# Decoder layer, cross-attention: the three score banks run on across batches

## What is computed

```python
def _L0_xattn_ref(q, k, v, gamma):          # per batch: q, k, v are (128, 512)
    h = 8                                    # N_HEAD, 16 rows each
    qh = q.reshape(B, h, dq, Lq); kh = k.reshape(B, h, dq, Lk); vh = v.reshape(B, h, dv, Lk)
    qk = jnp.einsum('bhdq,bhdl->bhql', qh, kh) * scale        # scale = 1/4
    sm = jax.nn.softmax(qk, axis=-1)                          # 512 x 512 per head
    ret = jnp.einsum('bhql,bhdl->bhdq', sm, vh)
    return gamma * ret.reshape(B, Dv, Lq)
```

## Time and profile before

| | us |
|---|---|
| median of three runs (lowest, highest) | 1818.55 (1813.82, 1830.88) |
| time of the profiled execution | 1817.9 |
| its span, from first to last instruction | 1816.0 |
| self-attention, about 0 to 608 us | 608 |
| cross-attention, about 608 to 1308 us | 700 |
| feed-forward, about 1308 to 1816 us | 508 |

### The profile page before, as it was taken

How to read it: one execution, slowest core, us unless ns; L and a number is a source line. 1 busy time by engine, 2 the same in 40 slices (tenths; PEclk the granted TensorE clock), 3 DMA queues, 4 the chain that set the end, 5 groups by cost and what they waited for, 6 DMA issues and landing times. The chain is left out here.

```text
span 1816.0 us, 35158 instructions
## 1 busy us (share of the span) xinstructions
PE 1609.2 (89%) x11937; PEld 874.9 (48%) x12000; DVE 1523.5 (84%) x1894; ACT 1329.7 (73%) x2821; POOL 1090.9 (60%) x1532
## 2 busy tenths in 40 slices
PE   6999999999998789999999999999858777777774
PEld 5777777777776333333333333333324333333332
DVE  5778888887887888999999899999568898989885
ACT  4666645555454478888888788888778888888893
POOL 6667667676765433255543555422467888888862
PEclk9999999999999699999999999999988888888887
DMA  4465443434346363445456554444233333333311
GB/s 146 140 193 166 130 116 118 130 104 139 107 128 178 101 118 94 118 116 120 109 158 162 152 126 115 109 118 118 90 117 97 112 106 113 105 107 109 111 47 41
DMA packets 119269, 217.10 MB, mean 120 GB/s; under 512 B 32241, under 2 KB 34705, under 8 KB 116785
## 3 DMA queue, kind: packets, MB, share of 16 engines
q1 hardware_dynamic: 110770, 213.64, 41.9%
q0 software_dynamic: 8320, 1.21, 0.4%
HBM read 137.67 MB, written 76.02 MB: 118 GB/s over the span
## 5 line engine op out<-in xcount | busy, mean ns | idle before, releaser
L969 DVE TENSOR_REDUCE b_smax<-wide 128x2 f32<-128x1024 f32 x512 | 620.6, 1225 | 63.4 <-PE wide L1029 51.3
L945 ACT ACTIVATE b_prob<-bank 128x512 f32<-128x512 f32 x1024 | 555.9, 599 | 113.0 <-PE bank L1076 103.6
L1076 PE MATMUL bank<-b_xs,b_cs 50*128 50x512 f32 x1024 | 329.5, 478 | 23.4 <-ACT b_prob L945 12.4
L1059 PE MATMUL sums<-b_prob,b_vT 128*32 128x256 f32 (+1 forms) x3584 | 318.7, 427 | 5.6 <-ACT b_prob L945 0.5
L1029 PE MATMUL wide<-b_cs,b_xs 48*128 48x512 f32 x1024 | 282.8, 437 | 9.1 <-DVE b_smax L969 7.7
L1076 PEld LDWEIGHTS bank<-b_xs,b_cs 50*128 50x128 f32 x1024 | 133.4, 187 | 233.9 <-ACT b_prob L945 170.7
L885 POOL TENSOR_SCALAR b_max_part<-b_neg_max 16x128 fp32r<-16x128 f32 x64 | 18.4, 288 | 325.2 <-ACT b_neg_max L936 325.2
L370 ACT ACTIVATE a_prob<-wide,a_neg_max 128x128 f32<-128x128 f32 x512 | 181.5, 417 | 2.5 <-DVE a_neg_max L461 2.5
L1986 PE MATMUL wide<-c_w,c_xqT 128*128 128x512 bf16 x482 | 159.3, 503 | 7.5 <-issue 7.5
L895 POOL DMA_DIRECT2D b_xs<-b_max_part x256 | 133.6, 527 | 42.1 <-POOL b_max_part L888 37.3
L1059 PEld LDWEIGHTS sums<-b_prob,b_vT 128*32 128x32 f32 x3584 | 72.8, 108 | 165.0 <-issue 107.5
(11 more groups left out here) (156 smaller groups left out, 3342.8 us busy)
## 6 DMA issues: line engine op xcount, KB each, us to landing
scratch_c_part<-a_c_part SPq DMA_DIRECT2D x64, 256.0 KB
scratch_x_part<-a_x_part SPq DMA_DIRECT2D x64, 256.0 KB
b_xs<-scratch_x_part SPq DMA_DIRECT2D x128, 128.0 KB, 3.1
b_cs<-scratch_c_part SPq DMA_DIRECT2D x128, 128.0 KB, 3.1
scratch_heads<-b_heads SPq DMA_DIRECT2D x64, 256.0 KB, 2.5
a_xT<-in_xT SPq DMA_DIRECT2D x32, 256.0 KB, 6.4
a_c_in<-in_ctx SPq DMA_DIRECT2D x32, 256.0 KB, 2.6
a_x<-in_x SPq DMA_DIRECT2D x32, 256.0 KB, 4.1
```

The lines of the kernel that those rows point to most:

```text
L945: act.activation(prob[k % 8][:, :], e_ps[bank_of(k)][:, :], ACT.Exp, scale=0.25).then_inc(exp_done, 1)
L969: dve.tensor_reduce(smax[g][:, :, j, qc], m_ps[u % 2][:, :, :], AX.X, ALU.max, negate=True).then_inc(max_done, 1)
L1059: last = pe.matmul(av_ps[2 * XD * h:2 * XD * (h + 1), cols], vT[p][:, lc, XG * g + h, :], prob[(XG * n + 2 * j + e) % 8][:, cols], start=( ...
L1076: pe.matmul(e_ps[bank_of(2 * u + e)][:, :], cs[p][g][half(e), j, lc * P:(lc + 1) * P], xs[p][g][half(e), j, :], start=True, stop=True).the ...
```

## The change

It touches two things and no instruction's place. The bank of a score unit is now counted through all batches, `bank_of(32 * t + k)`, on both sides (PE's matmul and ACT's exponential). The wait ahead of a pair or unit is the same formula for all: the first pair of a batch `t` waits for `exp_done >= 32 * t - 1`, so for all exponentials made before but the last one (unit 31 of the batch before); before it was `32 * t`. All other waits come out with the numbers they had. In the very first batch the count is not positive and there is no wait, as before. The lists of all five engines hold the same instructions in the same order, with waits on the same semaphores; one number per batch differs, and the bank addresses of batches whose 32 * t is not a multiple of 3.

```diff
-                    act.activation(prob[k % 8][:, :], e_ps[bank_of(k)][:, :], ACT.Exp, scale=0.25).then_inc(
+                    act.activation(prob[k % 8][:, :], e_ps[bank_of(UNITS * t + k)][:, :], ACT.Exp, scale=0.25).then_inc(
                         exp_done, 1)
...
-            free = max(2 * u + halves[-1] - 2, 0)
-            if free > 0 or not first:
-                pe.wait_ge(exp_done, UNITS * t + free)
+
+            free = UNITS * t + 2 * u + halves[-1] - 2
+            if free > 0:
+                pe.wait_ge(exp_done, free)
             for e in halves:
-                pe.matmul(e_ps[bank_of(2 * u + e)][:, :], cs[p][g][half(e), j, lc * P:(lc + 1) * P],
+                pe.matmul(e_ps[bank_of(UNITS * t + 2 * u + e)][:, :], cs[p][g][half(e), j, lc * P:(lc + 1) * P],
                           xs[p][g][half(e), j, :], start=True, stop=True).then_inc(score_done[e], 1)
```

## The result

The changed kernel took 1814.56 us in the median of 22 runs (1802.17 to 1829.51). The kernel before, run beside it, took 1826.07 us in the median of 22 (1813.82 to 1843.09; the three runs shown ahead of the prediction are among them). The ratio is 0.9941, with a 95% interval of 0.9916 to 0.9965: the kernel is faster by 0.6%. The ratios in this document are estimates from the single runs, those far above the fastest of their kernel left out; they can lie up to 0.003 away from the quotient of the two medians. The profiled execution of the changed kernel took 1802.17 us, the fastest of its 22, with a span of 1800.3.

What follows compares the result with a forecast made beforehand. PE in the cross-attention was taken as the bound; 26 batch starts at 0.48 us sum to 12.5 us, which off the median 1818.55 gives 1806.0 us, with a range of 1799 to 1815.

Steps and rivals of the forecast that it cites:

- What bounds the kernel: Cross-attention: PE is nearest to full, busy 670.2 of 700 us; its scores waited 12.4 us for exponentials in 28 waits.
- The price of the wait: At each of 26 batch starts, no longer waiting for the last exponential saves 0.48 us.
- The reading from the middle of the batch: Between steps 3 and 4, unit 4n+2 to next pair takes 1.28 us, against 1.76 at the batch's start.
- the idle column: Alternative measure from PE's idle time at batch starts: 26 x 0.45 = 11.7 us; the prediction used measured starts instead.
- What is late next: At a batch start the maxima's DMAs, step 7's products, DVE and ACT were checked; none was expected to hold PE.
- DVE's cover of 0.05 us: At a batch start DVE's reductions would end 0.05 us before the earlier plain scores; two buffers would hide slight lateness.
- The banks: Score banks change their number only; cost 0.
- The sum against the level of the runs: 26 x 0.48 = 12.5 us, taken off the three-run median 1818.55, gives 1806.0; a gain of 11 to 14 had chance 0.76.
- The five held places at gain 0: Five batch starts set by landings of the maxima's DMAs keep their time: gain 0, or up to 2.4 us if landings came earlier.
- a slower kernel: Rival: longer idle at held places lowers TensorE's clock, about 3.3 us each; four falls give 1819; chance 0.03.
- all held places would pay: Prediction's reading of the skill's rule: work after every DMA wait starts at half clock; trace agreed for batches 3 and 19.

Runs made afterwards that it cites:

- e2: Changed kernel with the full wait for all exponentials put back at each batch start, new banks kept: 1824.97 us, ratio 0.9983 to the kernel before.
- e3: Changed kernel with the full wait at the start and in the middle of every batch: 1842.26 us, ratio 1.0061 to the kernel before.
- e4: Changed kernel with the full wait ahead of the pair of all eight steps of a batch: 1891.72 us, ratio 1.0358 to the kernel before.
- e13: Changed kernel with the full wait back at each batch start, loads where they were, in the four-kernel job: 1820.83 us, ratio 0.9988 to the kernel before.
- e1: The changed kernel itself run again, in the job of the added full waits: 1813.10 us, ratio 0.992 to the kernel before.
- e9: Changed kernel with seven large loads sent one per batch and the feed-forward's first loads moved into batch 30: 1799.29 us, ratio 0.9842 to the kernel before.
- e14: The kernel of e9 (all large loads apart, new wait) run again in the four-kernel job: 1799.04 us, ratio 0.9875 to the kernel before.
- e10: The kernel of e9 with the full wait put back at each batch start: 1817.29 us, ratio 0.9953 to the kernel before.
- e15: The kernel of e10 (all large loads apart, old wait) run again in the four-kernel job: 1813.08 us, ratio 0.9943 to the kernel before.
- e12: The changed kernel run again in the four-kernel job, loads where they were: 1817.34 us, ratio 0.9959 to the kernel before.
- e7: Changed kernel with the weights' sums moved from GpSimd's DMA queue to SyncE's, large loads left in place: 1809.56 us, ratio 0.989 to the kernel before.
- e8: e5 and e7 together, large loads apart and the weights' sums by SyncE's queue: 1804.17 us, ratio 0.9863 to the kernel before.
- e6: The kernel of e5 with the full wait put back at each batch start: 1823.84 us, ratio 0.9984 to the kernel before.
- e5: Changed kernel with seven 1 MB feed-forward loads sent one per batch in batches 12 to 18: 1804.65 us, ratio 0.9872 to the kernel before.

## Why the prediction was right and wrong

**What bounds the kernel: right.** PE in the free batches, with one wait of 0.45 us of idle time, 0.48 to 0.50 by the starts. The waits that e2 and e3 add measure 0.50 and 0.49; only the eight of e4 cost less, 0.38 each.

**The price of the wait: right.** 0.48 was taken; the free periods went from 21.34 us to between 20.84 and 20.88. The reading from the middle of the batch (1.28 us from unit 4n+2 to the pair) came true to the digit. Going by starts rather than by the idle column was right too: the idle column would have said 0.45.

**What is late next: right.** Maxima, products, DVE and ACT all kept up at the free places; DVE's cover of 0.05 us was enough: from the first scores to the last the profile of the changed kernel lists one wait of PE for DVE, of 0.40 us in batch 0.

**The banks: right.** e2 against the kernel before: 0.9983 and, as e13, 0.9988, both with 1 inside the interval.

**The sum against the level of the runs: wrong, and this is the step that failed in absolute terms.** The prediction set 1806.0 by taking 12.5 us off 1818.55, "so the median after is 1806.0". The median of three runs was not the kernel's level: over 22 runs it is 1826.07, and over the other jobs' runs 1823.6 to 1828.7. From 1826.07 the same sum gives 1813.6, and 1814.56 was measured. Of the 8.6 us between 1806.0 and 1814.56, 7.5 are the level and 1.0 is the gain. That 1814.56 still lies inside the range of 1799 to 1815, by 0.4 us, is luck. The measured ratio of 0.9941 and the forecast one, 1806.0 over 1818.55 or 0.9931, agree within the interval. The gain over 22 runs, 11.5 us, is just short of the 12.5 forecast; the runs cannot tell these two apart. The three runs had a spread of 17 us, and the prediction used it for the range but not for its centre.

**The five held places at gain 0: the second weak step, its size open.** The prediction let them keep their time, because "neither end moves against the other". The waits there do move, in either kernel: over batches 14 to 19 those for the maxima's DMAs add up to 4.5, 4.2 and 4.2 us in three traces with the old wait and to 3.9, 4.8, 5.3 and 5.3 in four with the new one. What they cost moves more, by the clock, which the prediction had named as what makes such a wait dear and given 0.03 as the cause of a slower kernel. Slower it never was. Over these six batches its sum has a gain of 1.4 us (three free places); the traces show a loss of 3.3 on average, and a gain of 0.6 if e1 is left out. At the lower clock PE spent 6.8 us of these batches in each of the three traces with the old wait, and 0, 47.8, 13.7 and 13.7 us in the four with the new one. So that the falls are more frequent or longer with the new wait rests on four traces against three, of which one carries most.

The times say more. Over the single runs of all jobs the means are 1815.6 us (46 runs, new wait) and 1824.3 (24, old) with the loads where they were, 8.7 apart, and 1800.3 (12) and 1816.1 (24) with all of them apart, 15.8 apart. With 95% intervals from the scatter of the runs these are 8.7 within 3.4 and 15.8 within 3.5, so the gains differ by 7.1 within 4.9 us. With the 114 runs of the kernel before put to the old wait, the first is 10.4 within 2.4 and they differ by 5.4 within 4.3. About 1.7 us of either difference are plain: three or four more places gain 0.49 each. What is left for the held places to give back is 5.4 within 4.9 us or 3.7 within 4.3, with chips and jobs mixed in it: likely, and not shown. Why the landings should come later with the shorter batches is argued, not shown: the same bytes now share a shorter batch.

**Open.** With the loads apart the gain of the new wait came out at 14.0 to 19.2 us, where 29 or 30 places at 0.49 make 14.2 to 14.7. The traces show where the surplus is not. From the start of batch 4 to the start of batch 31 the kernels with all loads apart take 563.3 us with the new wait (e9 and e14) and 576.7 and 576.6 with the old (e10 and e15): 13.3 apart, 27 places at 0.49. And the longer idle time costs no clock there, which was e10's rival; e14 and e15:

```profile
700.00:1270.00 570.00, 564.44 (x4874) 215.67 (x4872) 542.18 (x492) 506.45 (x984) 257.25 (x378) 1.00 0.51 128
700.00:1270.00 570.00, 552.71 (x4753) 210.65 (x4753) 530.03 (x482) 494.19 (x960) 255.56 (x377) 1.00 0.51 126
```

What differs beyond that lies outside: over the 17 traces the stage up to the first scores, which no edit touches, took 608.2 to 622.4 us, and batch 0 took 22.3 to 30.3. So medians of 6 to 12 runs that scatter by some us are the nearest explanation; that it is only this, these runs don't settle.

## What to carry to other kernels

A wait that repeats inside a loop can be priced in the old trace, by finding a place in the same loop where the same list of instructions runs without it, and measuring from start to start. Before forecasting an absolute time, ask how well the runs know the level: here three runs were 7.5 us off, more than half of the effect. And look at the few places where the engine that bounds waits for a DMA: clearing them was worth another 14 us (1813.10 in e1, 1799.29 in e9, in two jobs) to 18 us (1817.34 in e12, 1799.04 in e14, side by side).

## What the runs showed of the hardware that was not expected

Many short idle times of PE don't lower its clock, one longer one may. Waits of PE and the window of 570 us in e4:

```profile
PE bank L1079 <- ACT b_prob L945: 81.0, 247, 0.5
```
```profile
700.00:1270.00 570.00, 504.46 (x4245) 187.74 (x4242) 474.34 (x430) 442.23 (x859) 237.68 (x335) 1.00 0.44 114
```

247 waits of up to 0.5 us in the cross-attention, 81 us of idle time in all, and the granted clock is 1.00 over the 570 us. A single wait of 2.40 us in e1 was followed by 31.5 us at 0.57, another of 4.89 in e12 by 31.5 us at 0.59, and one of 4.87 in the kernel before by a batch at 0.80. How long the clock stays down after nearly the same wait differs from run to run: batch 3 took 31.5 us after 4.89 us of waiting in e12 and 24.6 after 4.87 in the kernel before. The Trainium skill, page TensorE: Matmul & The Clock Gate, section HAM oscillation, says that waits for DMAs between stretches of matmuls make the work after them start at half clock. The traces agree for every wait of 1.87 us and more. The section's example has longer waits than any held place here but batch 3, so it doesn't say, as the prediction had it, that all held places would pay; in the kernel before only those of batches 3 and 19 did.

Of the waits between 0.9 and 1.8 us some were followed by a fall and some were not. After 1.58 us in e12 and again in e7 the next 20 us had 0.74 and 0.75, while 1.30 in the kernel before, 1.53 in the changed one and 1.73 in e12 left the clock at 1.00. The dearest of them was shorter than these. At the start of batch 31 in e8, and the window from there to the last scores:

```profile
1281.61 0.50 PE L1077 MATMUL bank<-b_xs,b_cs 50*128 50x512 f32 x2 [1.26 <-DMA b_xs<-b_max_part]
```
```profile
1281.61:1308.54 26.93, 26.41 (x137) 7.42 (x137) 7.38 (x15) 17.14 (x33) 13.17 (x26) 0.52 0.29 90
```

These 26.9 us were 17.9 in e9, where batch 31 isn't held. In e6 1.51 us at the same place were followed by 26.8 us at 0.53, and in e5 0.95 by 19.5 at 0.91, while 1.36 us in e13 cost no clock. So the length of a wait doesn't say here whether the clock falls. But from batch 4 to the last scores each of the 13 falls in the 17 traces comes at a wait for the maxima's DMAs or within 4.5 us of its end. The shortest such wait was 0.95 us. None comes at a wait for an exponential alone; these are all under 0.6 us.
